# Attention's planned order: sums only where two neighbouring steps are ready, scores up to five steps ahead, new hold constants

## What is computed

```python
# b = 4 batches, 16 heads of 16 numbers, t = 2048 tokens
q = concat([q_c, rope(q_e)]); k = concat([k_c, rope(k_e)])
scores = einsum('bhqd,bhkd->bhqk', q, k) / sqrt(16)
scores = where(causal, scores, -inf)
att = softmax(scores, axis=-1)
y = einsum('bhqk,bhkd->bhqd', att, v)
```

## Time and profile before

| | |
|---|---|
| time before, median of 3 runs | 2678.76 us |
| lowest and highest | 2668.99, 2687.64 us |
| span of the profiled execution | 2735.5 us |
| PE busy in it | 2406.9 us (88%) |
| DVE busy | 2048.1 us (75%) |
| ACT busy | 1581.1 us (58%) |
| POOL busy | 823.7 us (30%) |

### The profile page before, as it was taken

How to read it: one execution, slowest core, us unless ns; L and a number is a source line. 1 busy time by engine, 2 the same in 40 slices (tenths; PEclk the granted TensorE clock), 3 DMA queues, 4 the chain that set the end, 5 groups by cost and what they waited for, 6 DMA issues and landing times. The chain is left out here.

```text
span 2735.5 us, 48214 instructions
## 1 busy us (share of the span) xinstructions
PE 2406.9 (88%) x15842; PEld 1359.7 (50%) x15842; DVE 2048.1 (75%) x5002; ACT 1581.1 (58%) x2716; POOL 823.7 (30%) x1130
## 2 busy tenths in 40 slices
PE   6885799999999999999999999998777389998998
PEld 6774333333334333333334333332444278887897
DVE  3876989998999898888898998940355457765776
ACT  3663277777777776667777777776433234433443
POOL 1543011211212112111212112121055655555554
PEclk8997699999999999989999999997888689999999
DMA  3777814414504513504414423010675323323332
GB/s 145 261 260 212 113 39 63 74 42 61 86 29 64 86 34 59 84 27 65 83 35 64 80 44 71 8 31 20 236 203 177 94 92 113 107 93 96 111 109 72
DMA packets 147501, 255.95 MB, mean 94 GB/s; under 512 B 72951, under 2 KB 91897, under 8 KB 138916
## 3 DMA queue, kind: packets, MB, share of 16 engines
q1 hardware_dynamic: 114544, 164.96, 27.1%
q0 software_dynamic: 29904, 80.65, 8.9%
q10 hardware_dynamic: 2812, 7.26, 1.5%
HBM read 147.59 MB, written 107.76 MB: 93 GB/s over the span
## 5 line engine op out<-in xcount | busy, mean ns | idle before, releaser
L836 ACT ACTIVATE prob<-ps_s 128x512 f32<-128x512 f32 (+5 forms) x1620 | 1078.1, 714 | 480.5 <-PE ps_s L932 477.8
L857 DVE TENSOR_REDUCE maxes<-ps_m 128x2 f32<-128x1024 f32 x768 | 913.9, 1221 | 107.8 <-PE ps_m L973 104.8
L932 PE MATMUL ps_s<-q_st,k_st 50*128 50x512 f32 (+3 forms) x2560 | 610.2, 413 | 73.8 <-ACT prob L836 57.2
L973 PE MATMUL ps_m<-k_st,q_st 48*128 48x512 f32 (+3 forms) x2560 | 603.2, 443 | 75.9 <-DVE maxes L857 39.6
L953 PE MATMUL ps_o<-prob,v_sb 128*17 128x512 f32 (+3 forms) x5120 | 617.5, 556 | 1.2 <-ACT prob L836 0.7
L802 POOL TENSOR_SCALAR_AFFINE_SELECT prob<-prob 128x256 f32<-128x256 f32 x512 | 203.2, 406 | 1347.8 <-ACT prob L836 1220.8
L973 PEld LDWEIGHTS ps_m<-k_st,q_st 48*128 48x128 f32 x2560 | 272.6, 191 | 531.3 <-DVE maxes L857 256.6
L861 DVE CUSTOM_DVE_ANT_0 junk<-ps_m,causal 128x128 f32<-128x128 f32 (+3 forms) x1024 | 453.1, 484 | 44.2 <-PE ps_m L973 42.7
L932 PEld LDWEIGHTS ps_s<-q_st,k_st 50*128 50x128 f32 x2560 | 318.3, 190 | 306.1 <-ACT prob L836 234.1
L1728 ACT ACTIVATE h_hi<-ps_turned 128x512 fp32r<-128x512 f32 x142 | 85.0, 598 | 225.6 <-PE ps_turned L1843 157.9
L94 PE MATMUL ps_out<-experts_hi,h_lo 128*128 (+1 forms) x568 | 173.0, 305 | 0.0
(11 more groups left out here) (187 smaller groups left out, 3180.6 us busy)
## 6 DMA issues: line engine op xcount, KB each, us to landing
parts_dram<-parts SPq DMA_DIRECT2D x64, 512.0 KB, 3.8
q_st<-parts_dram SPq DMA_DIRECT2D x84, 256.0 KB, 8.5
k_st<-parts_dram SPq DMA_DIRECT2D x84, 256.0 KB, 18.4
v_dram<-v_out SPq DMA_DIRECT2D x16, 544.0 KB, 5.5
xin<-in_L_attn_x SPq DMA_DIRECT2D x16, 512.0 KB, 6.0
ffn_raw<-in_L_ffn_W POOLq DMA_DIRECT2D x32, 256.0 KB, 5.2
y_dram<-y_sb SPq DMA_DIRECT2D x64, 128.0 KB, 2.0
split_hi<-ffn_hi POOLq DMA_DIRECT2D x16, 512.0 KB, 3.2
```

Source lines behind the costliest of these rows:

```text
L836: last_exp = nc.scalar.activation(prob[:, at:at + n, lo:TB], bank[:, 0:n, lo:TB], ACT.Exp, scale=DH ** -0.5)
L857: return nc.vector.tensor_reduce(maxes[:, 2 * pair:2 * pair + 2, qt, kc], bank[:, :, :], AX.X, ALU.max)
L932: mm = nc.tensor.matmul(ps_s[k % 2][:, i, lo:TB], k_st[half(h % 2, ROWS), w % BUFS, h // 2, kt * P:(kt + 1) * P], q_st[half(h % 2, ROWS), ...
L973: mm = nc.tensor.matmul(ps_m[slot][:, i, 0:wide], q_st[half(i, STACK), w % BUFS, pair, qt * P:(qt + 1) * P], k_st[half(i, STACK), w % BUFS ...
```

## The change

`DEEP` goes from 3 to 5, `PROBS` stays at 6. A sum that would follow scores, a maximum or a turn (the array isn't in the "columns" mode), and isn't its chunk's last, is offered only when the groups of its own step and of the next one have been placed in the list, and not before the next step's exponential and mask are at most `PAIRED` = 820 ns away by the model. Once the array is in that mode, the next sum is offered as before. The four constants of `HOLD` are changed: the sum's goes from 0 to 158, those of maxima and scores from -171 and -140 to -239 and -243. No instruction is added or removed; the list is in another order.

```diff
-DEEP = 3
+DEEP = 5
+PAIRED = 820
 AHEAD = 2
 BUFS = 3
-HOLD = {"max": -171, "scores": -140, "sum": 0, "turn_out": -266}
+HOLD = {"max": -239, "scores": -243, "sum": 158, "turn_out": -293}
...
-        if s < len(STEP_LIST) and k > covers[s][-1]:
-            ready["sum"] = max(exp_done[covers[s][-1]] + 53, masked.get(s, 0.0) + 60,
-                               copied + 53 if STEP_FIRST[s] else 0.0)
+        if s < len(STEP_LIST):
+            second = s + 1 if mode != "columns" and not STEP_LAST[s] else s
+            if k > covers[second][-1]:
+                ready["sum"] = max(exp_done[covers[s][-1]] + 53, masked.get(s, 0.0) + 60,
+                                   copied + 53 if STEP_FIRST[s] else 0.0)
+                if second > s:
+                    ready["sum"] = max(ready["sum"], exp_done[covers[second][-1]] - PAIRED,
+                                       masked.get(second, 0.0) - PAIRED)
```

## The result

The change is slower: 2732.4 us (2724.2 to 2736.5) against 2673.9 us (2662.1 to 2687.6), medians of four runs each. The ratio is 1.0217, with a 95% interval of 1.0163 to 1.0271, so 58 us are lost where 34 were forecast as a gain.

A forecast was written before the change was run, and what follows sets the result against it. DVE was taken to pace the mixed part, with PE having room. Tail -42.8 us plus moved work 8.3 gave -34.5, other terms nothing: 2735.5 to 2701.0 profiled, 2644 us without a profile; range 2602 to 2700.

The forecast's parts named there:

- What bounds the kernel: Mixed part of attention: DVE sets the pace, losing one tenth of its time because PE brings the next bank late.
- The tail: After the last max piece: 63 fewer pieces of scores at 0.679 us each, saving 42.8 us.
- The cost of the moved work: Mixed part: 63 pieces and 12 sums add 25.1 us of PE work, of which a third, 8.3 us, shows.
- The order within the cycle: Mixed part, between users of `ps_m`: more long stretches but fewer ending in a sum; effect taken as zero.
- The second rival: Mixed part: 131 more long stretches starve DVE, 68 us, ending at 2704; chance 0.12 slower, 0.18 middle.
- its counter-argument: DVE in the mixed part: a full queue of two max pieces covers 2.44 us, against stretches of about 2.0.
- the sign that I had set for it: Profile after: DVE's waits for `ps_m` near 200 us instead of 134 would show that long stretches starve DVE.
- Pairs and depth: PE's list: 13 fewer turns, at most 3.7 us, and sums lagging further behind scores; both taken as nothing.
- the fifth rival: Mixed part: granted clock falls, 8 us per place; twelve such places cost 100 us and make it slower; chance 0.03.
- B: Theory in the follow-ups, mixed part: long stretches between users of `ps_m` starve DVE whatever the clock; e1 expected over 60 us slower.

The follow-up runs named there:

- e6: The kernel before, order unchanged, with the narrow diagonal matmuls of maxima and scores issued at all 512 columns: 2770.7 us against 2744.8, ratio 1.0128.
- e2: The change (DEEP 5, rule of the second step) with the old constants of HOLD: 2703.2 us against 2670.3 for the kernel before, ratio 1.0142.
- e5: The change, order unchanged, with narrow diagonal matmuls of maxima and scores at all 512 columns: 2780.3 us against 2744.8 for the kernel before, ratio 1.0167.
- e12: The change, with 344 groups of scores placed over 1600 ns behind the last sum multiplied twice: 2727.9 us against 2671.9 for the kernel before.
- e9: The change with HOLD's other constants back at the old values, only the sum at 158: 2798.4 us against 2744.8 for the kernel before.
- e10: The kernel before with DEEP 5, HOLD -230, -221, 1, -183, and the sum first after 2200 planner ns without one: 2652.7 us against 2671.9.

## Why the prediction was wrong

**What bounds the kernel** held in part. DVE's work is nearly the same, 1293 and 1301 us, and what changes is how long PE lets it wait. But PE was the busier of the two already by the prediction's own rows (1353 us against 1293), and its room was less than I took: in e6 56 us more of PE's busy time made the mixed part 43 us longer. DVE doesn't pace the part alone.

**The tail** held. 63 pieces fewer at 0.679 us were to give 42.8 us; the tail went from 124.9 to 79.3 us, 45.6 less, 0.655 us a piece. The lever is real in all orders, 0.61 to 0.68 us a piece from 106 to 248 pieces.

**The cost of the moved work** was set too low, if not by much. I took 8.3 us of 25, a third, as PE had room. DVE's idle time at full clock stayed at 130 us (132), but in a shorter time at full clock, its share going from 0.095 to 0.104. The split below leaves 10 us beside the clock, the part's length and DVE's own work, and the table's 0.2 us a piece gives 13 for 63 pieces. Within the 25 this is a matter of size and not what made the forecast fail.

**The order within the cycle**, which I left at zero, shows nothing at full clock: at 121 to 127 pieces in the tail, 219, 337 and 372 long stretches leave the same rest, +6, +3 and +8 us. The second rival had priced them with the mean of DVE's waits, 0.52 us. That a queue of two pieces covers them, as its counter-argument said, fits this. It had the direction (2704, 25 us slower) for a wrong reason, and the sign that I had set for it was met (DVE's waits near 200 us, measured 225), though it wasn't the cause: the sign couldn't tell it from the clock.

**Pairs and depth**: nothing, as taken, though a sum's waits for the exponential didn't go; they went from 9 to 16 us. The rule does matter with the old constants (e2), through what it leaves for the tail, which I had not looked for.

**The step that failed is the clock**, the fifth rival, chance 0.03: the sum had no term for the granted clock of the mixed part, which it put at nothing. I had its price about right: 8 us for a stretch of 40 at 0.79, which is 17 us at half clock in the record, so 0.47 us for each, where the runs give 0.31 to 0.37, and launches of one kernel 0.36 and 0.45. I took the mixed part's 0.98 as the argument that it was safe. But that 0.98 was a property of the order of before, in which a sum came at short distances. The change's list orders scores and maxima up to 401 ns ahead of it by the constants. 232 us more at half clock, at 0.32 us each, are 74 us of the 103 by which the mixed part grew. The rest of it is the longer part's own 0.10 (10 us), DVE's 9 us, and the 10 us that are left, the moved work's by the table: 103. The last term is what remains, so that the sum closes proves nothing. With -45.6 in the tail the sum is +57.

The prediction had a rule of the Trainium skill beside it (TensorE: Matmul & The Clock Gate, "A second HAM failure mode: psum-queue depth-cycling"), which puts a clock that falls and recovers again and again down to brief idling between groups of matmuls. The trace agrees with the pattern, 32 falls in the mixed part, and only in part with the cause: PE was idle for more than its average before the falls, but less in the change as a whole than before, 3% instead of 7%, with no gap over 0.7 us. What the runs add is the feeding: with the same order, more of it raises the clock again (e5, e6, e12). Another thing could have warned me: the planner's clock is a constant, `clock = 2.4`, so an order chosen by it can't see this cost.

**What stays open.** That the clock follows from feeding is shown by e5, e6 and e12, and its price by four readings that agree roughly (DVE's idle shares, e5 with e6, e9 with e2, and launches of one kernel). How much of the fall comes from sums that are late by the list and how much from TensorE's short waits isn't separated. e10 still has two stretches of 48 us at half clock in its profiled launch, which the timeline doesn't explain, and its own gain may depend on how often they come. B was not tried alone at over 400 long stretches, since the orders that have them also lack the lead. Each trace is one launch, and launches of the kernel before spread from 2643 to 2680 us on one chip alone, so differences of 10 or 20 us between two traces are weak.

## What to carry to other kernels

Before moving TensorE's dense work further apart, read the granted clock beside the order, and price each stretch at half clock: here it costs 0.3 to 0.4 us for each us. A mean clock of 0.98 says that the present order feeds the array, not that any order will. An engine that is busy for 93% of a part has little room: of the work added to it in e6 more than half came out, where the forecast took a third. Work moved out of a tail in which another engine is idle shortens the tail as counted; what is kept of it is small here. e10, with its sums close together and 12 to 16 pieces of lead from the third window on, ends half a per cent ahead.

## What the runs showed of the hardware

More matmul work in the same order raised the granted clock. In e5 all narrow matmuls of scores and maxima were widened, and the mixed part had 126 us at half clock instead of 297; in e12 344 groups were doubled, and it had 191. In the profiles the clock paid for the added work: attention took 1720 and 1726 us in the profiles, where the change took 1736, and neither kernel is clearly faster or slower than the change by the plain runs (ratios to before 1.0167 and 1.0268, the change's 1.0217, with intervals that overlap).

The part behind attention, the same in all kernels, takes 736 to 739 us on some chips and 798 to 801 us on another. A comparison of spans of two profiles from different chips (2731.4 and 2735.5 here) can hide a difference of 57 us.
